# Three mixing biases of a recurrent layer, computed in three column groups of TensorE and turned, instead of as single columns

## The reference

```python
# layer 1; x here is the normed input, xx one value per channel
xk = x * time_mix_k + (1.0 - time_mix_k) * xx
xv = x * time_mix_v + (1.0 - time_mix_v) * xx
xr = x * time_mix_r + (1.0 - time_mix_r) * xx
k = jnp.einsum('btc,oc->bto', xk, w_key)
v = jnp.einsum('btc,oc->bto', xv, w_value)
r = jax.nn.sigmoid(jnp.einsum('btc,oc->bto', xr, w_rec))
```

## Time and profile before

| | |
|---|---|
| Time, median of 3 runs | 840.95 us (840.45 to 841.15) |
| The profiled execution: time | 839.71 us |
| The profiled execution: span | 837.9 us |
| TensorE matmul / weight load busy | 826.0 us (99%) / 709.6 us (85%) |
| VectorE / ScalarE / GpSimd busy | 624.9 us (75%) / 478.4 us (57%) / 471.2 us (56%) |
| Granted TensorE clock | 1.00 over the span |

### The profile page before, as it was taken

The page is one execution under the profiler, slowest core; times in us unless marked ns, Lnnn a source line. Parts: engine busy times, 40 slices in busy tenths (PEclk is TensorE's granted clock), DMA queues, the critical chain, the costliest instruction groups (busy, mean ns, idle before and its releaser), DMA issues.

```text
span 837.9 us, 15615 instructions
## 1 busy us (share of the span) xinstructions
PE 826.0 (99%) x5436; PEld 709.6 (85%) x5436; DVE 624.9 (75%) x1267; ACT 478.4 (57%) x953; POOL 471.2 (56%) x327
## 2 busy tenths in 40 slices
PE   8999999999999999999999999999999999999998
PEld 7888888888867899999999888888889988876688
DVE  6899999999997665665567788687676785436767
ACT  3666666666674565655553475743453435367743
POOL 6676767677684855575757021019948316718820
PEclk9999999999999999999999999999999999999999
DMA  8101010000005385556313150011111010030001
GB/s 340 43 20 38 19 38 19 28 28 19 19 1 188 146 283 184 184 166 193 110 32 94 59 201 14 1 52 51 38 38 38 14 63 1 1 151 4 2 2 51
DMA packets 23345, 62.19 MB, mean 74 GB/s; under 512 B 3137, under 2 KB 13633, under 8 KB 20225
## 3 DMA queue, kind: packets, MB, share of 16 engines
q1 hardware_dynamic: 21760, 57.35, 19.8%
q0 software_dynamic: 1536, 4.20, 1.6%
HBM read 50.00 MB, written 8.39 MB: 70 GB/s over the span
## 4 chain that ended last, share of the span: by engine, by line
PE 88%; DVE 6%; POOL 2%; ACT 2%; issue 1%; DMA 1%; SPq 0%; DVEq 0%; POOLq 0%
PE banks L102 26%; PE banks L104 26%; PE banks L103 26%; PE banks L1387 3%; POOL arenaC L875 1%; PE banks L1373 1%; PE banks L1023 1%; PE banks L967 1%; PE banks L966 1%; DVE x L1457 1%; DVE arenaB L1892 1%; PE banks L888 1%; PE banks L1010 1%; PE banks L1056 1%; DMA arenaC<-in_wqkv 1%
## 5 line engine op out<-in xcount | busy, mean ns | idle before, releaser
L2153 ACT ACTIVATE banks<-banks,small 128x512 f32<-128x512 f32 x128 | 84.9, 664 | 70.8 <-DVE small L1522 70.8
L1522 DVE TENSOR_REDUCE small<-banks 128x1 f32<-128x512 f32 x128 | 86.7, 677 | 4.4 <-PE banks L104 4.4
L104 PE MATMUL banks<-arenaC_rounded,arenaD_rounded 128*128 128x512 f32 (+1 forms) x256 | 89.4, 349 | 0.0
L102 PE MATMUL banks<-xnT_rounded,arenaD_rounded 128*128 128x512 f32 x224 | 87.8, 392 | 1.1 <-POOL arenaC_rounded L741 0.9
L103 PE MATMUL banks<-s_tok_rounded,arenaD_rounded 128*128 128x512 f32 x224 | 87.2, 389 | 0.0
L104 PE MATMUL banks<-xnT_rounded,arenaD_rounded 128*128 128x512 f32 x192 | 74.8, 390 | 0.0
L104 PE MATMUL banks<-xnT_rounded,arenaC_rounded 128*128 128x512 f32 x192 | 74.7, 389 | 0.0
L102 PE MATMUL banks<-arenaC_rounded 128*128 128x512 f32 (+1 forms) x192 | 70.9, 369 | 1.2 <-DVE arenaC L1537 0.6
L1537 DVE SCALAR_TENSOR_TENSOR arenaC<-banks,small,arenaC 128x512 f32<-128x512 f32 x96 | 71.2, 741 | 0.0
L103 PE MATMUL banks<-arenaD_rounded,arenaC_rounded 128*128 128x512 f32 (+1 forms) x192 | 67.9, 354 | 0.0
L727 POOL TENSOR_TENSOR arenaD_rounded<-arenaC,ones 128x512 fp32r<-128x512 f32 x30 | 31.3, 1042 | 47.4 <-DVE arenaC L1537 46.5
(11 more groups left out here) (445 smaller groups left out, 2689.3 us busy)
## 6 DMA issues: line engine op xcount, KB each, us to landing
arenaD<-in_wexp SPq DMA_DIRECT2D x8, 1060.0 KB, 5.8
arenaD<-in_wexp SPq DMA_DIRECT2D x8, 1024.0 KB
arenaC<-in_wqkv SPq DMA_DIRECT2D x16, 384.0 KB, 3.0
arenaD<-in_wexp SPq DMA_DIRECT2D x8, 512.0 KB, 3.6
slots<-arenaB SPq DMA_DIRECT2D x1, 2560.0 KB, 9.9
arenaB<-in_sw SPq DMA_DIRECT2D x1, 2084.0 KB, 7.5
arenaC<-in_wo SPq DMA_DIRECT2D x1, 2048.0 KB, 15.3
arenaC<-slots SPq DMA_DIRECT2D x8, 256.0 KB, 3.2
```

Source lines behind the costliest of these rows:

```text
L102: pe.matmul(o, r(lhs[0]), r(rhs[0]), start=start, stop=False)
L104: return pe.matmul(o, r(lhs[1]), r(rhs[0]), start=False, stop=stop)
L1522: dve.tensor_reduce(negmax[:, n % 4:n % 4 + 1], bank[3 + n % 4][:, :], AX.X, ALU.max, negate=True).then_inc(max_done, 1)
L2153: act.activation(prob[r], prob[r], ACT.Exp, bias=negmax[:, r:r + 1], accum_out=rowsum[:, r:r + 1]).then_inc(exp_done, 1)
```

## The change

The three biases are computed in one go, with the roles of the operands exchanged. `mixed_biases` stands behind tile f = 1. It loads one column of `offs`, repeated 32 times, as weights, and moves the matrix's 256-wide rows through it. The three matrices go to three column groups of the array, so their results stand in partitions 0 to 31, 32 to 63 and 64 to 95 of bank 4, each as 32 equal rows of 256. VectorE copies these 96 rows to SBUF (`bias_rows`, in the buffer `rms`, which is free until layer 3). Behind tile f = 4, `turned_biases` waits for that copy and transposes it in two pieces of 96 partitions x 128. VectorE then picks six columns out of the turned rows where it read the six before. `bias_ready` now rises by three at once, and `bias_done` ends at 4 instead of 3.

```diff
+        bias_rows = rms[:, :, :].rearrange("p t g -> p (t g)")[0:96, :]
...
-            def mixed_bias(i):
-
+            def mixed_biases():
+
+                for c in range(DC):
+                    for i in range(3):
+                        mm = pe.matmul(bank[4][32 * i:32 * i + 32, 0:D], offs[:, i, c:c + 1].to_broadcast([P, 32]), w_rwkv[:, i, c, :],
+                                       start=(c == 0), stop=(c == DC - 1), tile_position=(0, 32 * i))
+                mm.then_inc(bias_ready, 3)
+
+            def turned_biases():
+
+                pe.wait_ge(bias_done, 3)
                 for o in range(DC):
-                    for c in range(DC):
-                        mm = pe.matmul(bank[4][:, 2 * i + o:2 * i + o + 1], w_rwkv[:, i, c, o * P:(o + 1) * P], offs[:, i, c:c + 1],
-                                       start=(c == 0), stop=(c == DC - 1))
+                    mm = pe.transpose(bank[4][:, D + 96 * o:D + 96 * o + 96], bias_rows[:, o * P:(o + 1) * P], ident[0:96, 0:96])
                 mm.then_inc(bias_ready, 1)
...
                 shared_hidden(0, f)
-                if f < 4:
-                    mixed_bias((0, 2, 1)[f - 1])
+                if f == 1:
+                    mixed_biases()
+                if f == 4:
+                    turned_biases()
             for f in range(2):
                 shared_hidden(1, f)
-            pe.wait_ge(bias_done, 3)
+            pe.wait_ge(bias_done, 4)
...
                     fold_rest(f)
+                if f == 1:
+                    dve.wait_ge(bias_ready, 3)
+                    dve.tensor_copy(bias_rows, bank[4][0:96, 0:D]).then_inc(bias_done, 1)
                 if f == 5:
-                    link(dve.tensor_copy(bias1[:, 0:3, :], bank[4][:, 0:6].rearrange("p (i c) -> p i c", i=3)))
+                    dve.wait_ge(bias_ready, 4)
+                    turned = bank[4][:, D:D + 192].rearrange("p (c i n) -> p i c n", c=DC, i=3)
+                    link(dve.tensor_copy(bias1[:, 0:3, :].unsqueeze(3), turned[:, :, :, 0:1]))
```

More of the change, by code:

```diff
@@ L1736, in combine @@
                         dve.wait_ge(rows_got[b], 16 * 2 * ST)
-                        dve.wait_ge(bias_done, 3)
+                        dve.wait_ge(bias_done, 4)
                     k, t = j // ST, ST * b + j % ST
@@ L2322, in gate_silu @@
                     act.activation(g[:, 2 * i:2 * i + 2, :], g[:, 2 * i:2 * i + 2, :], ACT.Silu).then_inc(silu_done, 1)
-            act.wait_ge(bias_done, 3)
+            act.wait_ge(bias_done, 4)
             gate_silu(0, (0, 1))
```

## The result

The changed kernel took 842.79 us (median of 14 executions, 841.55 to 844.05), the kernel before on the same chip 840.95 us (14 executions, 840.36 to 842.0). The ratio is 1.0021, with a 95% interval of 1.0014 to 1.0028. The change made the kernel slower by 1.8 us, where 1.2 us of gain was forecast. The traced execution took 843.3 us with a span of 841.5.

The account below looks back on a forecast made before the run. TensorE, busy for 99% of the span, was taken to bound the kernel: 2.71 us removed less 1.25 and 0.28 added gains 1.18, so the median goes from 840.95 to 839.8 us, range 839.1 to 841.0.

Parts of the forecast that it names:

- the first part: On TensorE, the six column-group matmuls with the steps into and out of them: 0.15 + 0.87 + 0.23 = 1.25 us added.
- The way in: On TensorE, time lost going into the run of column groups: 0.15 us, bounds 0 and 0.3.
- the way out: On TensorE, time lost coming out of the column groups to whole-array products: 0.23 us, bounds 0.13 and 0.35.
- The 2.38 of the Trainium skill: Reported speedup of three column groups over one; it would make the twelve records 1.08 us, but layer 3's row was preferred.
- The two transposes: On TensorE, the turning of the bias rows: 0.20 + 0.08 = 0.28 us added, bounds 0.2 and 0.4.
- The rival of less overlap: Column groups overlap less than in layer 3, so only 0.6 us gained, 840.3 us; 10 in 100.
- the cover that was forecast: VectorE's copy ends by 438.8 us, TensorE's transposes come at 440.8: 1.7 us or more, so waiting costs nothing.
- the path that was described: Layer 0's end: TensorE to ScalarE at 467.9 us, through VectorE to the norm at 481.3; TensorE's gain reaches the end.
- What does not move: GpSimd's gathers keep their own issue pace; TensorE waits for none of them, and no wait of its is for DMA.
- a new wait before 455 us: Sign that the prediction is wrong: TensorE shows a wait before 455 us that it did not have.
- It lies 1.24 us under the median of the runs: The profiled execution of 839.71 us against the 840.95 median, carried over to take the median to 839.8 us.
- The gain is given back later: Rival: the last `hS_split` or a gather comes late for TensorE, 0.4 to 1.2 us go, 840.2 to 841.0; 8 in 100.

Follow-up runs that it names:

- after_third: The changed kernel as it is, run once more on a chip where the kernel before takes 839.61 us; 838.22 us, ratio 0.9985.
- after_pad20: The changed kernel with forty already met waits, counted as twenty TensorE instructions, ahead of the first projection; 841.77 us, ratio 1.0016.
- batch 4: Runs sharing one chip (kernel before 840.9 us), including the changed kernel again, 843.72 us, and both kernels with longer warm-ups, 847.88 to 848.38.
- batch 5: Both kernels unaltered on another chip: the kernel before 839.61 us, the changed kernel 838.22 us, ratio 0.9985.
- after_half_gather: The changed kernel with the second sequence's eight gathers replaced by two plain loads of 1,024 rows; 838.47 us, ratio 0.9974.
- after_rows_late: The changed kernel with the first sequence's row products moved behind the second sequence's hidden tiles, VectorE's list reordered to match; 837.27 us, ratio 0.9975.
- after_pad128_again: The changed kernel with 32 more warm-up matmuls (128 records) at the start, timed a second time on another chip; 847.88 us, ratio 1.0094.
- after_pad64: The changed kernel with 16 more warm-up matmuls (64 records) at the start; 848.38 us, ratio 1.0094.
- after_slow: The changed kernel with two plain fp32 matmuls of 400 columns into an unused bank behind the column groups; 842.7 us, ratio 1.0028.
- batch 3: Runs sharing one chip (kernel before 839.52 us): both kernels with late row products, 838.87 and 837.16, and the changed kernel with more waits, 850.39 and 854.6.
- after_code64: The changed kernel with 128 already met waits (64 more TensorE instructions) ahead of the first projection; 850.39 us, ratio 1.0114.
- after_code128: The changed kernel with 256 already met waits (128 more TensorE instructions) ahead of the first projection; 854.6 us, ratio 1.0176.

## Why the prediction was wrong

**The local sum was right.** From the last product before the groups to the second behind them there are 437.39 - 435.74 = 1.65 us. Less two steps of 0.23 the first part costs 1.19 us, predicted 1.25. The run itself takes (1.06 - 0.385) / 3 = 0.225 us per round of three records, the last record's own 0.385 us taken off: four rounds, side by side, as in the earlier trace rows. The way in cost 0.09 us (0.32 less one step; taken as 0.15), the way out 0.20 (0.23). The 2.38 of the Trainium skill (TensorE: Matmul & The Clock Gate, "Measured speedup vs the span model"; its row is for 512 moving columns) was not seen here either: 12 records x 0.215 / (4 x 0.225) is 2.87. The two transposes cost 441.70 - 441.28 - 0.23 = 0.19 us, predicted 0.28. In all 2.71 - 1.19 - 0.19 = 1.33 us, predicted 1.18, and the steps between products gave 1.34. (The rival of less overlap counts the transposes as 0.35 us, which is neither the value of 0.28 nor the bound of 0.4; nothing hangs on it.)

**No new wait came from VectorE,** as forecast. Its copy and its last `hS_split` of the first sequence, on after_third:
```profile
438.58 0.42 DVE L1765 COPY rms<-banks 96x256 f32<-96x256 f32 x1
...
449.70 0.68 DVE L1725 TENSOR_TENSOR arenaB_rounded<-banks,arenaB_rounded 32x512 fp32r<-32x512 f32 x1
```
The copy ends at 439.0, 1.7 us ahead of the transposes, the cover that was forecast. The last split comes at 450.38 us, 1.6 us earlier than in the earlier trace rows. The next layer's norm, the end of the chain in the earlier trace rows, on after_third:
```profile
480.02 0.42 DVE xn L1483
```
It comes 1.32 us earlier than at 481.34. So the gain does reach the end, by the path that was described, and the span of 836.6 us is 1.3 below the 837.9 of before. For an execution like the one traced the prediction gave 838.5; the median was 838.22. And this gain was told from no change (interval 0.9976 to 0.9994), which the prediction's "about 0.2%" had held to be out of reach.

**The step that failed** is the one headed "What does not move": that GpSimd's gathers cost TensorE nothing since no wait of TensorE's is for a DMA. The gathers do cost TensorE time on some chips, without any wait for their data. The forecast named "a new wait before 455 us" as a sign; it came at 458. The same row of the changed kernel's chain, on the chip with holes, stands at 484.89, which is 3.55 us late where 1.3 was gained:
```profile
484.89 0.42 DVE xn L1483
```
4.34 of it arose in the row products (16.13 us instead of 11.79), and some 0.5 had come ahead of the change (435.04 against 434.51). Four gaps put down to issue hold 0.59 + 0.44 + 0.71 + 0.33 = 2.07 us of the 4.34. The rest is late starts too short to be counted as idle, and the half clock. By after_pad20, which lost 3.86 us at full clock, the half clock is probably the smaller part.

**The clue was in the prediction's own sum.** "It lies 1.24 us under the median of the runs" was added as a constant to get from the traced execution to the median. All three runs of before, and later all fourteen, lay above the traced one, by 0.65 us at least. A trace that is faster than every timed run is of an execution that did not have something which the others had. Most likely this was the small form of the holes, some 1.2 to 1.4 us (inferred, as said above). With the change the holes are of the large form on such chips: 842.79 - 838.22 = 4.6 us in the result, and 843.72 - 838.22 = 5.5 in batch 4, against the quiet chip of batch 5. None of the rivals was this case. "The gain is given back later" came nearest, with the gathers as one of its causes and 841.0 as its upper end.

**What is shown, and what is open.** Shown: the change gains 1.4 us on a quiet chip, and 1.7 us in the other order; the holes appear with the second eight gathers under way and 256-column products running, not without the former (after_half_gather), and not when 512-column products stand through most of that time (after_rows_late on quiet chips only, so for this last part the test is weak, since there the changed kernel in its own order had none either). Shown too: one program has the holes on one chip and none on another, with and without the change. Of the gathers, it is more likely the packets than GpSimd's own work, since the last hole comes after GpSimd's last gather instruction has ended (by 1.3 us in the changed kernel); no run separates the two. Not shown: what is short. The holes end 1.41 to 1.46 us apart, sometimes with one more in between, four or five products from one to the next, with no data awaited; the last gathers follow each other every 1.30 us, so the holes don't keep the gathers' step. A late supply of TensorE's instructions would look like this. The traces record when code is loaded (16,384 bytes at a time on the queue of kind "instruction"), and in two traces none falls among the holes: in the changed kernel the loads around them stand at 441.76 and 465.48 us, in after_pad128_again, whose holes lie between 465.6 and 469, at 459.61 and 483.73. (In after_pad64 one does, at 464.81.) So the holes need no load of code under way; whether instructions come late for another reason isn't recorded. Open as well is why the changed kernel's holes begin 8.6 us in and not 10.4 or later, which made 1.2 us into 4.6. after_slow, with the gained time given back, still began at 8.8 us, so it is not the start time alone; after_pad128_again began at 10.2, with only the code shifted, so the place has some part in it, though it didn't account for the holes in batch 3. And after_code64 and after_code128 had holes on a chip whose times for the kernel before (839.52) are those of a quiet one, which no theory here explains.

## What to carry to other kernels

Matmuls with one moving column and many weight loads cost their loads; exchanging the operands and putting independent ones into column groups made 2.71 us into 1.38 here, and the estimate from rows of another stage held within 0.15 us. Compare the traced execution's own time with the timed runs before using it as a base: where all runs lie on one side of it, something that the trace does not show belongs to the kernel, and a gain upstream can change its size. Where a change matters by less than such an effect, time it on more than one chip, and look for an order that takes the long run of narrow products out of the gathers' way (here that order was tried on quiet chips alone).

## What the runs showed of the hardware

While indirect gathers ran, TensorE had gaps of 0.20 to 0.78 us with no wait named, four or five products apart, in runs of 256-column products of 0.118 us each (11.79 us for 100 records), on some chips and not on others. The 512-column products of 0.23 us, which ran under the first eight gathers in every trace, showed none. Plain loads at 324 GB/s under the narrow products (after_half_gather) made none either. The gaps took the granted clock to 0.50 for some 3.4 us in one trace of the changed kernel and 6.8 in the other (the time at 0.50 that gives each window its mean), and it stayed there for 2 to 5 us after the last gap. It did not always fall: in the windows of after_pad20 and after_pad128_again, with four and three such gaps, it stayed at 1.00. Waits that were already met cost 54 ns each (128 more of them delayed the next product by 6.94 us); forty in the same place (after_pad20) cost nothing, since the product behind them started at 10.14. The median of the kernel before differed by up to 1.5 us (0.18%) from chip to chip, that of the changed one by 4.6 to 5.5 us (0.6%).
